# Perceiver layer on one core: the last context blocks, the order of the drain, table fetch, paired adds and the loop for the rest

## The reference, cut to what matters

```python
x = x + xattn(layernorm(x), ctx, ctx, mask, gamma, beta)   # softmax(x ctx^T / sqrt(512)) ctx, normed
x = x + attn(layernorm(x), W_qkv, W_out)                   # within each batch of 64
# xf = layernorm(x), 1024 x 512
scores = xf @ router_w.T
top_v, top_i = top_k(scores, 2); routing_w = softmax(top_v)
for e in range(8):
    w_e = sum(where(top_i == e, routing_w, 0))
    out += gelu(xf @ w1[e].T) @ w2[e].T * w_e
```

## Time and profile before

| | |
|---|---|
| time, median of 3 runs | 818.93 us (818.65 to 818.98) |
| profiled execution | 821.06 us; span 819.4 us |
| busy | PE 741.8, weight loads 553.1, DVE 448.0, ACT 305.0, POOL 150.7 us |
| mean clock granted | 0.957 of full speed |
| drain and first fetch | from 330.8 (end of the last sums) to 390.07 us |
| expert stage, then tail | 390.07 to 794.07, then to 819.4 us |
| 1 MB loads, median to landing | context 22.7, expert weights 5.0 us; largest of all lines: mask 26.7 us |
| DRAIN on L221 | POOL 6.28 us; SP, ACT, DVE, PE 8 to 17 ns |

### The profile page before, as it was taken

One profiled execution on the slowest core, in us unless ns is written; L12 is line 12 of the kernel. 1 busy time (PEld: TensorE's weight loads), 2 busy tenths in 40 slices (PEclk: granted clock), 3 DMA queues, 4 the chain that ended last, 5 costly groups with the idle time before them and its releaser, 6 DMA issues.

```text
span 819.4 us, 12383 instructions
## 1 busy us (share of the span) xinstructions
PE 741.8 (91%) x4626; PEld 553.1 (68%) x4626; DVE 448.0 (55%) x1052; ACT 305.0 (37%) x508; POOL 150.7 (18%) x172
## 2 busy tenths in 40 slices
PE   5999999999999997951999999999999999999970
PEld 3453445444545453630999999999998998888860
DVE  4143568676766736575457454555556565655410
ACT  2040122212112113220555355555565656566410
POOL 2133031231404010015201111111211211100000
PEclk9999999999999999965899899999999999999995
DMA  9999999999999979011354354646656666665101
GB/s 343 402 418 390 408 399 379 422 384 422 383 394 397 415 320 411 36 52 32 93 199 162 112 167 160 185 158 209 179 208 182 208 203 224 215 192 191 25 6 20
DMA packets 35517, 198.81 MB, mean 243 GB/s; under 512 B 4830, under 2 KB 5309, under 8 KB 14465
## 3 DMA queue, kind: packets, MB, share of 16 engines
q1 hardware_dynamic: 29680, 187.81, 60.4%
q0 software_dynamic: 5056, 9.09, 6.3%
q10 hardware_dynamic: 720, 1.10, 0.4%
HBM read 188.14 MB, written 9.85 MB: 242 GB/s over the span
## 4 chain that ended last, share of the span: by engine, by line
PE 76%; DMA 9%; DVE 6%; issue 3%; SPq 2%; ACT 1%; POOL 1%; DVEq 0%; POOLq 0%
PE ps L765 8%; PE ps L727 8%; PE ps L951 8%; PE ps L953 7%; PE ps L952 7%; PE ps L973 4%; PE ps L975 4%; PE ps L974 4%; PE ps L981 4%; PE ps L980 4%; PE ps L982 4%; DMA arena<-in_w_out 3%; DMA arena<-in_ctx_turned 3%; PE ps L780 3%; DMA arena<-in_ctx 2%
## 5 line engine op out<-in xcount | busy, mean ns | idle before, releaser
L442 POOL TENSOR_TENSOR small<-small 128x1 f32<-128x1 f32 x64 | 13.2, 206 | 604.0 <-issue 122.3
L953 PE MATMUL ps<-xT,low_a 128*128 128x288 f32 (+5 forms) x384 | 111.2, 290 | 0.0
L1442 DVE TENSOR_TENSOR h_ring<-hid,h_ring 128x288 fp32r<-128x288 f32 (+5 forms) x128 | 55.6, 435 | 97.7 <-ACT h_ring L1137 97.7
L1132 ACT ACTIVATE hid<-ps 128x288 f32<-128x288 f32 (+5 forms) x128 | 50.6, 395 | 151.3 <-PE ps L953 148.8
L765 PE MATMUL ps<-arena 128*64 128x512 f32 (+1 forms) x416 | 96.2, 607 | 5.3 <-DMA arena<-in_ctx 4.1
L1333 DVE TENSOR_TENSOR low_a<-w_raw_a,high_b 128x2048 fp32r<-128x2048 f32 x32 | 73.2, 2291 | 36.9 <-ACT high_b L1072 36.9
L1025 ACT COPY arena<-ps 128x512 f32<-128x512 f32 (+2 forms) x93 | 43.9, 528 | 120.4 <-PE ps L702 68.0
L727 PE MATMUL ps<-arena 128*64 128x512 f32 x384 | 85.5, 596 | 0.8 <-DMA arena<-in_ctx_turned 0.6
L951 PE MATMUL ps<-xT,high_b 128*128 128x288 f32 (+5 forms) x256 | 74.9, 292 | 0.0
L953 PEld LDWEIGHTS ps<-xT,low_a 128*128 128x128 f32 x384 | 73.6, 192 | 0.0
L952 PE MATMUL ps<-xT,high_b 128*128 128x288 f32 (+5 forms) x256 | 73.4, 287 | 0.0
(11 more groups left out here) (192 smaller groups left out, 1621.5 us busy)
## 6 DMA issues: line engine op xcount, KB each, us to landing
arena<-in_ctx_turned SPq DMA_DIRECT2D x48, 1024.0 KB, 22.2
arena<-in_ctx SPq DMA_DIRECT2D x48, 1024.0 KB, 22.7
w_raw_a<-in_w SPq DMA_DIRECT2D x48, 1024.0 KB, 5.0
w_raw_b<-in_w SPq DMA_DIRECT2D x16, 1024.0 KB, 4.9
arena<-in_mask SPq DMA_DIRECT2D x8, 800.5 KB, 26.7
arena<-in_w_qkv SPq DMA_DIRECT2D x3, 1024.0 KB, 9.6
arena<-in_ctx SPq DMA_DIRECT2D x16, 130.0 KB
out<-res SPq DMA_DIRECT2D x8, 256.0 KB, 22.3
```

The costliest lines, as they stand in the source:

```text
L953: mm = pe.matmul(o, w_low[2 * f][:, cols], high[:, k, 0:w.width], start=False, stop=(k == KC - 1))
L1132: nc.scalar.activation(hid[:, c % 2, 0:w.width], bank(c % UP_BANKS)[:, 0:w.width], ACT.Gelu).then_inc(gelu_done, 1)
L1442: dve.tensor_tensor(h_ring[:, c % RING, 1, 0:w.width], hid[:, c % 2, 0:w.width], h_ring[:, c % RING, 0, 0:w.width].bitcast(F32), ALU.subtr ...
```

## The change: what it does

1. **Last context blocks.** `ctxb` of tile 7 goes into the places of `ctxT` (`ctxb_last`), each pair behind the scores of tile 7 on that block, with semaphores of its own. The raw weight blocks 0 to 5 go where `ctxb` lay, each pair behind the sums of tile 6; blocks 6 and 7 follow the sums of tile 7 on block 0. The stores of tile 5 come behind all of these on SP.
2. **Drain.** PE, ACT and DVE take tile 6's pieces further ahead of tile 7's. DVE subtracts weight blocks 0 and 1 between `route_first(5)` and `route_second(5)`, where all four stood behind the ordering of experts.
3. **Tables in one piece.** `fetch` takes all entries of a window with one DMA; `ahead` has four places instead of three.
4. **Turns of window 0** use banks 7, 3 and 4 and don't wait for `low_x`.
5. **Adds in pairs.** Two semaphores, one for each of the two buffers; POOL waits at the start of a window for all earlier adds and not between the adds of one window. A wait for all stands at the end.
6. **Loop.** `more` is read behind window 1 (POOL: ahead of the last two windows' adds), and one test `more > 0` stands around the loop.

```diff
-                    ("u", LAST), ("pt", LAST), ("xr", LAST - 1), ("out", LAST), ("logit", LAST - 1), ("xr", LAST),
+                    ("u", LAST), ("xr", LAST - 1), ("pt", LAST), ("logit", LAST - 1), ("out", LAST),
...
+def adds_before(w, half):
+
+    if w.turn is None:
+        return (w.at(PER_TILE) + 1 - half) // 2
+    return STATIC_ADDS[half] + (w.turn if half == 0 else 0)
+
+
+STATIC_ADDS = [(sum(PER_TILE[:EXPERTS]) + 1 - half) // 2 for half in range(2)]
+
+
+def turn_bank(w, t):
+    return TURN if w.kind or t == 0 else UP_BANKS + t - 1
...
-        with (nc.sbuf_tensor("before_b", [P, 13312], F32), nc.sbuf_tensor("w_raw_b", [P, 2, WBLK], F32) as w_raw_b,
-              nc.sbuf_tensor("before_a", [P, 8192], F32), nc.sbuf_tensor("w_raw_a", [P, 6, WBLK], F32) as w_raw_a):
+        with (nc.sbuf_tensor("before_raw", [P, 13312], F32), nc.sbuf_tensor("w_raw_a", [P, 6, WBLK], F32) as w_raw_a,
+              nc.sbuf_tensor("w_raw_b", [P, 2, WBLK], F32) as w_raw_b):
...
+        ctxb_last = [view(25600 + i * 4096, 2, 4, D) for i in range(NBLK - 1)]
...
-                if p >= 1:
+                if p == LAST:
+                    sp.wait_ge(scored, scored_at(LAST, blk))
+                elif p >= 1:
                     sp.wait_ge(pv_block, summed_at(p - 1, blk))
                 for b in range(2):
-                    sp.dma_start(ctxb[blk][:, b, :, :],
+                    sp.dma_start((ctxb_last if p == LAST else ctxb)[blk][:, b, :, :],
                                  ctx_in[2 * p + b, blk * BLK:(blk + 1) * BLK, :].rearrange("(p c) d -> p c d", p=P)
-                                 ).then_inc(ctx_here[blk], 16)
+                                 ).then_inc((ctx_last_here if p == LAST else ctx_here)[blk], 16)
...
-                    if r == LAST:
-                        sp.wait_ge(scored, scored_at(LAST, blk))
-                        load_block(sp, 0, 2 * blk)
-                        load_block(sp, 0, 2 * blk + 1)
-                    if blk == NBLK - 2 and runs(r - 2):
+                    if r < LAST and blk == NBLK - 2 and runs(r - 2):
                         store_sum(r - 2)
                     load_ctx(r, blk)
                     if blk == 0 and runs(r + 2):
                         load_mask(r + 2)
                         load_rest(r + 2)
+                if r == LAST:
+                    for blk in range(NBLK - 1):
+                        sp.wait_ge(pv_block, summed_at(LAST - 1, blk))
+                        load_block(sp, 0, 2 * blk)
+                        load_block(sp, 0, 2 * blk + 1)
+                    store_sum(r - 2)
                 if runs(r - 2):
                     store_token(r - 2)
+            sp.wait_ge(pv_block, summed_at(LAST, 0))
             for j in range(6, WB):
...
-                for t, (a, m) in enumerate(w.tiles):
-                    pool.dma_start(ahead[w.ring][t][0:m, :], slots_m[bass.ds(row + a, m), :]).then_inc(m_here, 16)
+                n = len(w.tiles)
+                pool.dma_start(ahead[w.ring][:, 0:n, :], slots_m[bass.ds(row, n * P), :].rearrange("(t p) d -> p t d", p=P)
+                               ).then_inc(m_here, 16)
                 wait_past(pool, x_turned, w.at(PER_TILE))
-                pool.wait_ge(m_here, w.at(PER_TILE, len(w.tiles)) * 16)
+                pool.wait_ge(m_here, w.at(PER_WINDOW, 1) * 16)
                 for t, (a, m) in enumerate(w.tiles):
                     carry_pool_waits(pool, rows, 27)
                     pool.indirect_dma_start(
                         out=xg[t][0:m, :], out_offset=None, in_=tokens_x,
-                        in_offset=bass.IndirectOffsetOnAxis(ap=ahead[w.ring][t].bitcast(I32)[0:m, 1:2], axis=0)
+                        in_offset=bass.IndirectOffsetOnAxis(ap=ahead[w.ring][:, t, :].bitcast(I32)[0:m, 1:2], axis=0)
                     ).then_inc(x_here[t], 16)
 
             def add(w):
 
+                for half in range(2):
+                    wait_past(pool, added[half], adds_before(w, half) * 16)
                 for t, (a, m) in enumerate(w.tiles):
                     pool.wait_ge(y_ready, w.at(PER_TILE, t + 1))
                     carry_pool_waits(pool, own)
                     pool.indirect_dma_start(
-                        out=acc, out_offset=bass.IndirectOffsetOnAxis(ap=ahead[w.ring][t].bitcast(I32)[0:m, 1:2], axis=0),
-                        in_=yb[yb_of(w, t)][0:m, :], in_offset=None, compute_op=ALU.add).then_inc(added, 16)
-                    pool.wait_ge(added, w.at(PER_TILE, t + 1) * 16)
+                        out=acc, out_offset=bass.IndirectOffsetOnAxis(ap=ahead[w.ring][:, t, :].bitcast(I32)[0:m, 1:2],
+                                                                      axis=0),
+                        in_=yb[yb_of(w, t)][0:m, :], in_offset=None, compute_op=ALU.add).then_inc(added[yb_of(w, t)], 16)
...
+            pool.wait_ge(more_ready, 1)
+            more = in_use(pool)
             add(STATIC[-2])
             add(STATIC[-1])
-            pool.wait_ge(more_ready, 1)
-            more = in_use(pool)
...
+            with pool.If(more > 0):
+                with pool.Fori(0, MORE) as i:
...
+            for half in range(2):
+                pool.wait_ge(added[half], STATIC_ADDS[half] * 16)
...
+            turn_second(LAST - 1)
             turn_own_probs(LAST)
-            turn_second(LAST - 1)
+            router(LAST - 1)
             weigh(LAST)
-            router(LAST - 1)
+            ranks(LAST - 1)
             turn_second(LAST)
...
-                wait_past(pe, x_ready, w.at(PER_TILE, t))
+                if w.kind:
+                    pe.wait_ge(x_ready, w.at(PER_TILE, t))
+                o = bank(turn_bank(w, t))
                 for k in range(KC):
-                    mm = pe.transpose(bank(TURN)[:, k * P:k * P + m], xg[t][0:m, k * P:(k + 1) * P], ident[0:m, 0:m])
+                    mm = pe.transpose(o[:, k * P:k * P + m], xg[t][0:m, k * P:(k + 1) * P], ident[0:m, 0:m])
...
+                if w.kind == 1:
+                    pe.wait_ge(more_ready, 1)
+                    more = in_use(pe)
...
-            split_high(STATIC[0], 2)
-            copy_fill("g", LAST - 1, gT, shown=by_chunk)
-            copy_fill("u", LAST - 1, uu)
-            own_exps(LAST - 1)
             copy_fill("g", LAST, gT, shown=by_chunk)
             own_exps(LAST)
             copy_fill("u", LAST, uu)
             copy_fill("xr", LAST - 1, xrT, shown=by_chunk)
+            split_high(STATIC[0], 2)
+            gate_exp(LAST - 1)
+            copy_fill("xr", LAST, xrT, shown=by_chunk)
             split_high(STATIC[0], 3)
-            copy_fill("xr", LAST, xrT, shown=by_chunk)
-            gate_exp(LAST - 1)
             gate_exp(LAST)
...
             route_first(LAST - 2)
+            for j in range(2):
+                split_low(STATIC[0], j)
             route_second(LAST - 2)
             attended(LAST)
+            tops(LAST - 1)
             first_norm(LAST)
-            tops(LAST - 1)
+            copy_pt(LAST - 1)
             dve.wait_ge(filled, filled_at("xn", LAST))
             dve.tensor_copy(xnT, bank(bank_at("xn", LAST)).rearrange("p (k t) -> p k t", k=KC)).then_inc(copied[False], 1)
-            copy_pt(LAST - 1)
+            second_norm(LAST - 1)
             tops(LAST)
-            second_norm(LAST - 1)
             copy_pt(LAST)
+            route_first(LAST - 1)
             second_norm(LAST)
-            route_first(LAST - 1)
+            route_second(LAST - 1)
             route_first(LAST)
-            route_second(LAST - 1)
             route_second(LAST)
...
-            for j in range(4):
+            for j in range(2, 4):
```

152 lines of the change are left out of this document (81 added, 71 removed).

## The result

| | before | after |
|---|---|---|
| median (range, runs) | 818.95 us (818.65 to 819.75, 4) | 801.60 us (800.69 to 801.91, 4) |
| ratio, 95% interval | | 0.9772, 0.9753 to 0.979 |
| span of the profiled execution | 819.4 us | 800.3 us |
| DRAIN of POOL at the end | 6.28 us | 5.30 us |
| mean clock granted | 0.957 | 0.970 |

The account below looks back on a forecast made before the run. PE was taken as busy for 400.39 of the expert stage's 404.00 us, so gains were priced where PE waits or has ended: 5.1 + 2.1 + 3.1 + 7.3 = 17.6 us, giving 801.3 us, range 797.5 to 808.5.

Parts of the forecast that it names:

- Context and DVE's start: Last sums: PE's 2.47 us context wait goes; DVE starts tile 7 at 329.5 instead of 330.99, leaving 1.5 us.
- Reordering by itself 0: Drain: tile 7's places ready at 367.7 against 367.6, so the new order alone gives 0, bounds -1.5 and +1.8.
- POOL: Behind the drain: tile 6's earlier sends and one table DMA land the first rows at 378.4, gaining 5.1 us.
- The hold: POOL beside the two late DVE subtractions: instructions reading SBUF are held; without this up to 1.0 us better.
- Three banks: First turns of window 0: own banks cut turn to first up matmul from 6.56 to 4.4, gain 2.1 us.
- Expert stage 0: Same matmuls and early reads covered by queued work: 0, at most 0.8 us; DVE's count and half clock stay.
- Tail: Program end: adds in pairs gain 3.1 us; read and branch ahead of the last landing gain 7.3 us.
- DRAIN from 802.5: Sign at the end: POOL's closing DRAIN starts at 802.5 and takes about 6.3 us.
- rival A: POOL's DRAIN waits on the last software DMA, ending at 815.8; sum 10.6 us, time 808.3; chance 0.13.
- B: Clock rival, half clock behind DVE's count: spared, 798.3 us, or falling again elsewhere, 804.3; together 0.07.
- C: Front gives little, DVE late by 1.5, landing and table slow by 2.7: gain 3 of 7.2, 805.5 us; chance 0.10.
- D: Slower: raw weight blocks land late, holding the two subtractions ahead of tile 7 on DVE; 820 us and more; chance 0.02.

Follow-up runs that it names:

- e1: Changed kernel, but POOL waits for each add of a window to land before issuing the next: 805.42 us, ratio 0.9818.
- e9: Changed kernel with DVE's small instructions that plan the rest spread over window 0, four at a time: 796.47 us, ratio 0.9699.
- e3: Changed kernel with a table DMA for each tile again, 20 DMAs instead of 8: 804.05 us, ratio 0.9806.
- e2: Changed kernel without the one test around the loop for the rest, on every engine; early read kept: 802.18 us, ratio 0.9773.
- e6: Changed kernel with the last context blocks and raw weights in their old places and SP's old order, new drain order kept: 804.0 us, ratio 0.9825.
- e5: Changed kernel with the old drain order on PE, ACT and DVE, all four subtractions behind the ordering, contexts in new places: 803.71 us, ratio 0.9797.
- e10: Changed kernel with tile 6's second turn and router ahead of tile 7's values, two subtractions in DVE's gaps: 800.21 us, ratio 0.9747.
- e7: Changed kernel with all four weight subtractions behind the ordering of experts, nothing else changed: 803.45 us, ratio 0.9794.
- e4: Changed kernel with all first turns on one bank, each waiting for the subtraction of the tile before: 804.01 us, ratio 0.9799.
- e11: Changed kernel with the edits of e9 and e10 together: 794.94 us, ratio 0.9679.
- e12: As e11, but with the tables fetched by SP's queue, so POOL issues 56 DMAs: 795.57 us, ratio 0.9691.
- e8: Changed kernel with 21 more small DMAs on POOL, three for each of seven windows, data unused: 803.68 us, ratio 0.9803.

## Why the prediction was right, step by step

The sum was 17.6 us; the spans differ by 19.1, the medians by 17.35. The profiled execution of after took 801.9 us where I had 803.4, but it lies only 0.3 over its median, where I had assumed 2.1 as before. The two misses nearly cancel, so 801.3 against 801.6 is closer than the terms were, and that is luck. Forecast and measured in the spans: front 7.2 and 7.7, expert stage 0 and 0.3, adds 3.1 and 3.0, read and loop 7.3 and 7.1, DRAIN 0 and 1.0.

*Context and DVE's start.* Right, and for the reason given: the wait went, and DVE's queue took a part of it back. DVE started tile 7 at 329.10 (forecast 329.5). The sums ended at 326.76, not 328.4: the same 20 matmuls in front of them took 4.51 us where the execution of before showed 6.21. That is the clock: before had it at half from 315.2 to 318.6, and 9 of the 14 profiles show such a fall, with either kernel's front. It comes and goes, and does not belong to the change. It mattered little, because DVE was late anyway: with the same front the first up matmul is at 382.50 and 382.55 in e1 and e9, which had the fall, and at 382.36 and 382.52 in after and e3, which had not. Only in e2, where the half clock lasted 6.8 us, was it at 384.08. e6 puts the contexts at 1.6 us with the subtractions in front.

*Reordering by itself 0.* In the sense meant (places of tile 7) right: 365.77 plus 1.76 is 367.53 against 367.6 before. Keys 339.63 (340.1), second norm 353.77 (354.0), turn 358.01; the router of tile 6 and its routing stood in front of tile 7 as said. e5, which keeps the old order and has all subtractions late, lost 2.7 us, all through POOL. e10 shows what the new order had left: 1.2 to 2.8 us, by the clock.

*POOL.* Sends 367.95 and 369.24 (368.2, 369.5), table 371.62 (371.7 to 372.8), gather 374.57 (375.0), first turn 378.06 (378.4): 5.45 instead of 5.1 us. The step's inner split was wrong: I counted 0.9 us for the table in one piece (3.3 to 2.4), e3 measured 0.3. One DMA of three tiles takes 0.84 us to issue, not 0.65, the wait behind it is 1.58 us against 1.22 in e3, and the next instruction was held for 0.2: 2.95 us from issue to gather.

*The hold.* I said that it cost up to 1.0 us. In after it cost 0.2: POOL's L459 at 374.04 took 0.37 where 0.19 is normal, and the gather began just as the last subtraction ended. What it costs where it hits is larger: 2.9 us in e7, and in e5 sends of 2.86 and 1.87. I had booked the gain on POOL on tile 6's entries going early. The runs show 2.7 us as soon as the two subtractions stand late, in the new order (e7) as in the old (e5); what the early sends are worth by themselves is not shown. By the rule of the Trainium skill ("SBUF — State Buffer", "Who interferes with whom") the gather is held and the table fetch is not, as the latter only writes SBUF. The trace agrees: 2.89 against 1.02 us for a gather, and in e3 the three table fetches beside a subtraction (369.84, 4.49) took 0.56 each.

*Three banks.* 4.30 us from turn to up (forecast 4.4); e4: 2.27 (2.1).

*Expert stage 0.* The reads of `more` took PE 484 ns at 494.8 with no idle time of the array. The half clock behind the stall was 3.4 us long instead of over 6, but the stage began with 5.4 us at half clock instead of 3.6, which took back most of that; it gained 0.3 us in all. So the 0 came out of two shifts of the clock that I had not forecast. The prediction left the stall itself alone ("stays"); it was the largest thing to be had in the stage, 5.0 us (e9, e11).

*Tail.* Adds 3.0 (3.1; e1: 3.2). Read and loop 7.1 (7.3), and e2 shows that my sentence "stand in front of the landing" is the cause, not the test, which a reader of the diff would name first. Landing 8.6 us behind the last matmul (8.4). The sign "DRAIN from 802.5" was given in the old times; less the 7.2 us of the front it is 795.3, and the DRAIN began at 794.7.

*The DRAIN, the step that was mis-sized.* I took 6.28 us as fixed; it is 5.30, and rival A had it tied to the last DMA's issue, which would have made it 13. Neither: it goes with how many DMAs POOL issued, a count that the tables in one piece lowered from 76 to 64.

| kernel | DMAs issued by POOL | DRAIN, ns | ns for each |
|---|---|---|---|
| e12 | 56 | 4648 | 83.0 |
| after, e1, e2, e4 to e7, e9 to e11 | 64 | 5302 | 82.8 |
| before | 76 | 6282 | 82.7 |
| e3 | 76 | 6373 | 83.9 |
| e8 | 85 | 7017 | 82.6 |

In e1 the last add is issued 5.3 us behind the first, in after 1.95, and the DRAIN is the same. In e12 the tables are still fetched, by another queue, and it is shorter. The Trainium skill has it as a constant of about 12 ns on all five engines ("VectorE: DVE Perf Modes", "The DRAIN you can't avoid"); for POOL the runs disagree, and they decide. DVE's, too, took 1095 ns in after, right behind its last instruction, where it took 17 before. So the tables in one piece, for which I gave 0.9 us at the front, were worth 0.3 there and 1.0 here. It is the number of DMAs that counts and not their bytes: e3's 20 table DMAs move 134.5 KB where after's 8 move 160, and its DRAIN is 1.07 us longer. What POOL does in this time no trace shows.

*Rivals B, C and D.* B: the clock behind the stall was at half for less long, not spared. The fall at 315 us, which of the two profiles only that of before had, should make none of the difference: PE waited 2.47 us behind it for a context block whose load was issued at 308.92, ahead of the fall, and would only have waited longer without it. C: no; the last send is at 369.24. D: the raw blocks were there when ACT was free, since the casts start at 320.99, right behind its last small operation.

The parts, each undone alone, are contexts 1.6 and order with subtractions 2.7 (at the first up matmul), banks 2.3 (from first turn to up) and tables 0.3 (at the gather): 6.9 of the 7.7 us.

## What to carry to other kernels

- At a program's end, put reads of registers and loops that may be empty ahead of the wait for the last transfer, not behind it: here that was 7 us, and the test that skips the loop 0.2.
- A long two-input instruction on DVE belongs where DVE waits and POOL does not gather: two of the four subtractions cost 2.9 us behind the ordering (e7), and in DVE's gaps they held only a send that nobody waited for (e10). And a row of small instructions that an engine runs between two chunks of a steady stage was seen as a stall of PE of 3.2 us with half clock behind it; four at a time between chunks, PE was idle for 0.4 us in the whole stage.
- Price the parts in the trace, and compare executions whose clock did the same: one edit was 2.8 us between two profiles without the fall, 1.2 between two with it, and 1.4 to 2.1 in the medians.

## What was not expected of the hardware

POOL's closing DRAIN took 83 ns for each DMA that POOL had issued in the whole program, however long ago, from 56 to 85 of them. Fifteen empty turns of the loop take POOL's sequencer 6.2 us (789.8 to 796.0), 0.44 each. One table DMA for three tiles took 0.84 us to issue against 0.56 for one tile.
